# Two GNN layers on one core: the next batch's record work moved to the end of every engine's step, the sort ahead of the ranks, and 30 of 50 plain tiles read by one-hots

## The reference

```python
# layer 0
h = relu(layernorm(x))
x = x + segment_sum((h * node_vec1)[src], dst) * node_vec1_n2
# layer 1
h = relu(layernorm(x))
x = x + (1 + eps) * h + segment_sum(relu(h[src] + edge_attr), dst)
```

## Time and profile before

| what | value |
|---|---|
| median of 3 runs | 5049.15 us (5040.99 to 5050.13) |
| profiled execution | 5051.24 us, its span 5049.3 us |
| granted TensorE clock, mean | 0.899 of full speed |
| PE busy | 3734.7 us (74%) |
| DVE busy | 4209.4 us (83%) |
| POOL busy | 3745.2 us (74%) |
| ACT busy | 2165.5 us (43%) |
| layer 0, start of the first to end of the last direct step | about 160 to 3250 us of the span |

### The profile page before, as it was taken

How to read it: one execution, slowest core, us unless ns; L and a number is a source line. 1 busy time by engine, 2 the same in 40 slices (tenths; PEclk the granted TensorE clock), 3 DMA queues, 4 the chain that set the end, 5 groups by cost and what they waited for, 6 DMA issues and landing times.

```text
span 5049.3 us, 126723 instructions
## 1 busy us (share of the span) xinstructions
PE 3734.7 (74%) x43516; PEld 2830.1 (56%) x43516; DVE 4209.4 (83%) x13149; ACT 2165.5 (43%) x5783; POOL 3745.2 (74%) x3759
## 2 busy tenths in 40 slices
PE   0678878888878787888888888826666667776665
PEld 0455555565555555655555655526666666666664
DVE  9778888888888888888888888658888888888887
ACT  1344544444544454444444444423333333333332
POOL 6777777777777777777777777657777777777774
PEclk9999999999999999999999999968888888888887
DMA  6222222222222222222222221122112222222221
GB/s 105 52 52 53 52 53 52 53 52 53 52 53 52 53 52 53 52 53 52 53 52 53 52 52 29 27 68 55 48 49 53 54 55 55 55 55 55 55 55 25
DMA packets 438712, 266.11 MB, mean 53 GB/s; under 512 B 331484, under 2 KB 422732, under 8 KB 431632
## 3 DMA queue, kind: packets, MB, share of 16 engines
q1 hardware_dynamic: 317976, 185.11, 16.3%
q0 software_dynamic: 118496, 66.60, 7.5%
q10 hardware_dynamic: 1560, 5.60, 0.3%
HBM read 177.53 MB, written 79.52 MB: 51 GB/s over the span
## 4 chain that ended last, share of the span: by engine, by line
POOL 33%; DVE 22%; PE 22%; issue 18%; DMA 3%; ACT 1%; DVEq 1%; POOLq 0%; SPq 0%; ACTq 0%
POOL stage L683 24%; PE candidates L1096 14%; POOL records L693 6%; DVE arena L1534 6%; DVE arena L1515 3%; PE plain_ps L1108 3%; DVE counts L1293 2%; DMA record<-records 2%; PE candidates L1011 1%; POOL message L676 1%; PE key_rows L993 1%; DVE rank L1319 1%; DVE counts L1313 1%; DVE record L1599 1%; PE sorted_agg L1039 1%
## 5 line engine op out<-in xcount | busy, mean ns | idle before, releaser
L693 POOL DMA_INDIRECT records<-stage,place_i x1875 | 1896.8, 1012 | 607.6 <-issue 571.4
L683 POOL DMA_INDIRECT stage<-table,src_plain x1250 | 1247.4, 998 | 402.7 <-issue 380.6
L872 ACT ACTIVATE message<-candidates,member_is 128x96 bf16<-128x96 f32 x3360 | 852.1, 345 | 860.2 <-PE candidates L1096 859.9
L1534 DVE TENSOR_SCALAR arena<-window_iota,dst_rel 128x224 bf16<-128x224 f16 (+1 forms) x5000 | 1145.8, 302 | 46.0
L802 ACT ACTIVATE arena<-key_rows 125x640 f16<-125x640 f16 x1000 | 650.8, 708 | 708.6 <-DVE arena L1515 352.9
L1039 PE MATMUL sorted_agg<-arena 128*96 128x224 bf16 (+1 forms) x5000 | 629.7, 278 | 191.7 <-DVE arena L1534 191.3
L1515 DVE TENSOR_SCALAR arena<-arena,row_key 125x1280 bf16<-125x1280 f16 x1000 | 565.6, 566 | 177.7 <-ACT arena L802 138.0
L993 PE MATMUL key_rows<-ident,record 128*125 128x128 f16 x5000 | 417.4, 237 | 395.1 <-DMA record<-records 219.4
L676 POOL DMA_INDIRECT message<-table,mid_src x528 | 534.0, 1011 | 185.9 <-issue 155.4
L1039 PEld LDWEIGHTS sorted_agg<-arena 128*96 128x96 bf16 x5000 | 518.7, 132 | 219.4 <-DVE arena L1534 217.7
L993 PEld LDWEIGHTS key_rows<-ident,record 128*125 128x125 f16 x5000 | 380.8, 152 | 416.9 <-issue 330.4
(11 more groups left out here) (196 smaller groups left out, 4555.1 us busy)
## 6 DMA issues: line engine op xcount, KB each, us to landing
record<-records SPq DMA_DIRECT2D x50, 1650.0 KB, 7.2
stage<-in_edge_attr SPq DMA_DIRECT2D x125, 400.0 KB
records<-pad SPq DMA_DIRECT2D x25, 1650.0 KB
records<-stage,place_i POOLq DMA_INDIRECT x1875
stage<-table,src_plain POOLq DMA_INDIRECT x1250
message<-table,mid_src POOLq DMA_INDIRECT x528
xs<-in_x SPq DMA_DIRECT2D x8, 390.6 KB
table<-parts ACTq DMA_DIRECT2D x4, 585.9 KB
```

The source lines that it names most:

```text
L683: pool.indirect_dma_start(message[:, k, j, :] if l == 0 else rows[:, k, j, :], None, table0 if l == 0 else table1, bass.IndirectOffsetOnAx ...
L693: pool.indirect_dma_start(records, bass.IndirectOffsetOnAxis(ap=place_i[:, h, e:e + 1], axis=0), stage[:, h, e, :], None).then_inc(scatter ...
L872: last = nc.scalar.activation(direct_message[n % DB][:, m * WIDE:(m + 1) * WIDE], candidates[n % 2][:, m * WIDE:(m + 1) * WIDE], ACT.Copy, ...
L1534: last = nc.vector.tensor_scalar(dst_onehot(g, t), window_iota[:, 0:WA if tile == 0 else WT], dst_rel[:, h, tile:tile + 1], None, ALU.is_e ...
```

## The change

`BOUNDS` gets a fifteenth entry (14), so there are 30 direct tiles and 20 mid tiles; the steps hold five tiles each, and the two "arena" steps begin with a tile of 14 matmuls. The sort of batch b+1 takes the place of `rank_within` of batch b+2, which goes to where the sort stood. `prefixes` and `copy_prefix` go from the beginning of the last direct step to its last tile. On TensorE the turns of the next batch's keys leave the last direct tiles and stand behind them and behind `join_pair`; on ScalarE the copies of these keys stand behind `copy_pair`; on DVE `first_onehots` of the next batch stands behind `rank_places` and `add_pair`.

```diff
-    BOUNDS = (6, 7, 8, 8, 9, 9, 10, 10, 11, 11, 12, 12, 13, 13)
+    BOUNDS = (6, 7, 8, 8, 9, 9, 10, 10, 11, 11, 12, 12, 13, 13, 14)
-    STEPS = ((LOW, range(4, -1, -1), "far"), (LOW, range(13, 9, -1), "arena"), ...
+    STEPS = ((LOW, range(4, -1, -1), "far"), (LOW, range(14, 9, -1), "arena"), ...
 # ACT, step0
-                            if n == FIRST[5] and left_after(b) >= 2:
+                            if n == DIRECTS - 1 and left_after(b) >= 2:
                                 copy_prefix(b + 2)
-                            if n in (DIRECTS - 3, DIRECTS - 2):
-                                copy_keys(*after(b, h, u), n - (DIRECTS - 3))
...
                         copy_pair(b)
-                    if not is_last(b):
+                        copy_keys(*after(b, h, u), 0)
+                        copy_keys(*after(b, h, u), 1)
                         copy_candidates(*after(b, h, u), 0)
 # PE, step0
-                            if n == FIRST[5] and left_after(b) >= 2:
+                            if n == DIRECTS - 1 and left_after(b) >= 2:
                                 prefixes(b + 2)
                             pick_wide(b, n)
...
-                            if n in (DIRECTS - 3, DIRECTS - 2):
-                                turn_keys(*after(b, h, u), n - (DIRECTS - 3))
                         direct_products(b, DIRECTS - 1)
+                        join_pair(b)
+                        turn_keys(*after(b, h, u), 0)
+                        turn_keys(*after(b, h, u), 1)
                         pick(*after(b, h, u), 0)
-                        join_pair(b)
 # DVE, step0
                         wide_onehots(b, 4)
                         if more:
-                            rank_within(b + 2, h, u + 1)
+                            sort_rows(b + 1, 1 - h)
                         direct_onehots(b, h, 4)
                         wide_onehots(b, 5)
                         direct_onehots(b, h, 5)
                         if more:
-                            sort_rows(b + 1, 1 - h)
+                            rank_within(b + 2, h, u + 1)
                             rank_sums(b + 2)
-                        first_onehots(*after(b, h, u))
-                        if more:
                             rank_places(b + 2, h, u + 1)
                         add_pair(b)
+
+                        first_onehots(*after(b, h, u))
```

10 lines of the change are left out of this document (5 added, 5 removed).

## The result

| kernel | median | range | runs |
|---|---|---|---|
| before | 5049.64 us | 5040.99 to 5055.92 | 4 |
| changed | 5377.81 us | 5376.82 to 5379.43 | 4 |

The ratio is 1.0649 [1.0636, 1.0661]: slower by 328 us. The forecast was 5430 us, range 5350 to 5520, with 94% for slower. The sign, the place and the size of the main term were right; the forecast is 52 us too long, and nearly all of that is one term, the turn of the hardware loop from one round to the next.

The account below looks back on a forecast made before the run. It took two locked cycles, POOL's transfers and one step's compute chain through DVE and PE, as the bound. Longer steps gave +366 us, the layer's start +16.6, its end -3: +379 on 5051.2, so 5430 us, range 5350 to 5520.

Parts of the forecast that it names:

- The step's length within a round: Layer 0, prefix sums to the next prefix sums without a loop turn: 125.2 + 16.6 = 141.8 us.
- Two tiles: Direct tiles on PE, which has no idle time there: two more direct tiles lengthen each step by 6.6 us.
- the copy behind four more tiles: Prefix copy on ACT, now behind the step's last tile: the sums on DVE start 10.0 us later.
- The 28.1 us behind the sums: DVE from prefix sums to the group loop's first source one-hots: the total stays 28.1 us within a round.
- the third rival: PE resumes at half clock for some of the groups, 3 us a step: 5505 us; chance 11%.
- The loop's turn: Layer 0 where the loop turns round: 9.3 us extra, 8.0 plus 1.3 of a second wait, making a 151.1 us step.
- the branch 10 us on top: PE at the loop's branch: it stops 10 us each time, 9 times, with bounds of 0 to 10.
- Behind the last sums: Last prefix sums to the first gather: 143.9 us becomes about 141, so -3; the last batch and layer 1 cost 0.
- The record and POOL: PE's 7.65 us wait for the record goes in layer 0; POOL waits 15 to 25 us ahead of each scatter.
- POOL as the bound: Rival: POOL holds the cycle and all else fits under it, steps of 124.5 us, 4943 us; chance 4%.
- Two tiles only: Rival: only the two tiles cost, the four tiles' wait being hidden at the step's end; 5150 us; chance 8%.
- The exchange of sort and ranks: DVE, sort (10.4 us) and ranks (14.0 us) change places: the sum of its work stays the same, no cost.

Follow-up runs that it names:

- a1: The changed kernel, but with the 28 direct and 22 mid tiles of before: 5226.3 us, ratio to before 1.0347.
- b2: The kernel before, with 30 direct and 20 mid tiles only: 5156.18 us, ratio 1.0216.
- b1: The kernel before, with only the prefixes and their copy moved to the step's last direct tile: 5403.97 us, ratio 1.0707.
- b3: The kernel before, with only the next batch's key turns, key copies and first one-hots moved last: 5035.16 us, ratio 0.9976.
- b4: The kernel before, with only the next batch's sort moved ahead of the ranks on DVE: 5138.57 us, ratio 1.0181.
- a2: The changed kernel, with prefixes and their copy back at the beginning of the last direct step: 5289.97 us, ratio to before 1.0473.
- a4: The changed kernel, with the next batch's key turns, key copies and first one-hots back where before has them: 5410.7 us, ratio to before 1.0713.
- a3: The changed kernel, with 3.3 MB a batch of extra writes behind the ranks on SyncE's queue: 5977.24 us, ratio to before 1.1834.
- c1: The kernel before, with keys last and the loads of batch b+2 late: 8931.8 us on a chip where before took 8830.86 us, ratio 1.0113.
- c2: As c1, with 39 small matmuls (156 PE instructions) added in front: 8929.78 us on the same slow chip, ratio to before 1.011.
- b5: The kernel before, with loads and fills of batch b+2 held until the third group: 8841.03 us on the slow chip, ratio 1.0012.
- b6: The kernel before, with 39 small matmuls (156 PE instructions) ahead of the first batch: 8835.16 us on the slow chip, ratio 1.0003.

## Why the prediction was right, and where its size was off

**The step's length within a round: right, and for the reason given.** Two tiles +6.8 in a1 and +6.7 in b2 (forecast 6.6). The sums come 16.5 us later in the first step, and so does the step's length within a round; what is left, 9.8, is the copy behind four more tiles (forecast 10.0). a1 has these 9.8 us alone: its steps of 135.0 us against 125.2. DVE idles 10.6 us for it (forecast 10 to 14).

**The 28.1 us behind the sums: right.** Within a round 1741.44 - 1713.39 = 28.05 us pass from the sums to the group loop's first source one-hots:

```profile
1741.44 1.20 DVE L1514 TENSOR_SCALAR arena<-arena,row_key 125x1280 bf16<-125x1280 f16 x2
```

with no wait ahead of them. That PE picks late costs nothing there, and the half clock on PE's return, the third rival, adds nothing within a round either: the groups keep their 33.30 us, at a granted clock of 1.00.

**The loop's turn: the term that was mis-sized.** The prediction had "the branch 10 us on top" and "a second wait ... of which 1.3 is extra: 9.3 us where the loop turns round". Measured, it is 144.95 - 141.7 = 3.2 us. From sums to one-hots it is 1885.68 - 1855.12 = 30.6 us where 36.1 were forecast, and the second wait is not there. The nine turns take 1307.0 us in all where 1359.9 were forecast, the step that leaves the loop 141.3 where 143 were, and the twelve others 1701.5 where 1701.6 were. Together that is 54.7, the whole gap in the stretch of the sums, 3204.5 - 3149.8.

Two things in the term were wrong. The first is the size of PE's stop, 2.3 to 4.0 us in the nine turns in place of 10. The second is what bounds there. In the prediction's sum PE's chain does, with DVE waiting for the keys. Measured from the sums' start, PE begins to pick at 20.8 us (forecast 21.6) and resumes behind the branch at 24.9 (33.8), and the first keys are copied at 27.1. But DVE has destination one-hots to make until 27.9 (1883.00). So a stop of PE of 2.28 us is hidden behind DVE's work, and what lengthens the turn is DVE's own branch, 2.68 us, for which the prediction had no term. b1 and b2 have this stop of DVE in all nine turns too, 2.7 to 3.1 us, with "issue" as its releaser. Where PE's stop is longer, it shows: in a1 PE stands for 5.91 us, and the turn is 4 to 5 us longer than a step within a round.

Why is PE's stop shorter than the row of 10.00 us? The trace has the branch itself, `COMPARE_BRANCH` in L455. The view of that line gives, for PE's ten branches of layer 0, the shortest, median and longest duration in ns, before and after. The shortest is that of the tenth, which leaves the loop.

```profile
L455 PEldq COMPARE_BRANCH  x10: 83/7350/7610, 682.0 to 3000.1; - x10
```

```profile
L455 PEldq COMPARE_BRANCH  x10: 83/4696/5149, 730.1 to 3313.9; - x10
```

From the start of a taken branch to the next matmul there are two parts, the instruction and what follows it. The table has them in us for all kernels on the first chips, nine turns each; the share is that of the DMA engines over the whole of it:

| kernel | to the next matmul | the instruction | what follows | DMA share | code of |
|---|---|---|---|---|---|
| before | 9.4 to 11.1 | 6.2 to 7.6 | 3.1 to 3.8 | 0.57 to 0.63 | 28 tiles |
| b3 | 8.5 to 10.7, once 13.2 | 4.3 to 7.5 | 3.1 to 3.8, once 8.9 | 0.42 to 0.67, once 1.08 | 28 tiles |
| b4 | 7.9 to 10.8 | 4.5 to 7.6 | 3.3 to 3.9 | 0.40 to 0.62 | 28 tiles |
| b1 | 6.4 to 7.4 | 3.4 to 3.9 | 3.0 to 3.5 | 0.03 | 28 tiles |
| a1 | 7.0 to 7.6 | 3.5 to 3.9 | 3.3 to 3.9 | 0.08 to 0.10 | 28 tiles |
| b2 | 4.1 to 7.3 | 3.8 to 7.0 | 0.3 | 0.46 to 0.70 | 30 tiles |
| after | 3.8 to 5.4 | 3.4 to 5.1 | 0.3 to 0.4 | 0.08 to 0.13 | 30 tiles |
| a2 | 3.7 to 4.2 | 3.4 to 3.9 | 0.3 | 0.08 to 0.09 | 30 tiles |
| a4 | 3.7 to 5.4 | 3.4 to 5.1 | 0.3 | 0.02 to 0.05 | 30 tiles |
| a3 | 4.3 to 6.8 | 4.0 to 6.5 | 0.3 | 0.89 to 1.22 | 30 tiles |

What follows the instruction depends on where the loop's code lies. That is shown: 156 instructions in front of the same code take it from 3.2 to 3.6 us down to 0.3 (c1 to c2, which differ in nothing else, and b5 to b6, which differ in the time of the loads too). It is 3 us or more in all five kernels of 28 tiles and 0.3 in all five of 30, so the longer code of two more tiles does here what the shift does; of the 7.7 us between the stops of 10.00 and 2.28 this part is some 3. The instruction itself takes 3.4 to 5.1 us where the DMA engines are quiet, and up to 7.6 where their share is 0.4 or more. That is a correlation, not shown as the cause: a3 was to make it and gave only 1.1 us more than after, and the run that was to take it away (b5) fell on a chip where these engines are quiet at the branch without it (share 0.13 to 0.17 in b6).

The Trainium skill ("Runtime: NRT & Kernel Launch", Instruction fetch mechanics) says that a taken branch to a far target stalls on an instruction fetch. That the wait depends on the code's place, with the same work around it, agrees. The 0.1 us for a compare-and-branch in the Trainium skill ("Advanced Engine Details and Errata", Control Flow Timing), which the prediction weighed, agrees with the instruction where PE leaves the loop (0.083 us) and with DVE's (0.055 to 0.072), but not with PE's taken branch (3.4 us and more), nor with the 2.7 us for which DVE stands behind its own. By it the forecast would have been 5358, nearer to the result than mine, but only by luck: it has no stop at all on either engine.

**Behind the last sums: forecast -3, measured +0.6.** To the first plain gather it is 3574.97 - 3434.06 = 140.9 us against 143.9, so the -3 came as forecast. The rest of the execution, costed at nothing, is 3.7 us longer. Its code is the same, and among the kernels on the first chips it varies by 13 us, so nothing is read from that.

**The record and POOL: right.** PE's wait for records is gone and POOL waits 15 to 23 us ahead of the first scatter, once 13.7 (forecast 15 to 25). DVE's waits for the prefixes are 242.9 us in all, a little under the 250 to 300 of the forecast.

**The rivals.** POOL as the bound (4943): no; it waits for the places in every step. Two tiles only (5150): true of b2 alone, where the copy stands early; refuted for the whole by DVE's 10.6 us. Half clock (5505): not in the groups. But where a stop of some 4 us falls ahead of a direct tile, as in a2 and b4, the clock does cost, 1.7 us in the rows shown. The prediction was lucky there: with the prefixes late this stop does not arise.

**The exchange of sort and ranks** was costed at nothing. That DVE idles 10.6 us ahead of the sums speaks for it, but no run takes the exchange alone out of the changed kernel, so it is not shown. And it is no free move: alone it costs 91 us (b4), and in a2 its stop of 5.8 us stands against the 10.0 that an early copy would give.

## What to carry to other kernels

In a list that is held in order on each engine, ask for each cross-engine handover what stands ahead of the releasing instruction: here a 0.32 us copy, moved behind four tiles of others' work, costs 10 us in each of 23 steps (9.8 measured), though this move adds no work. A part that is moved can close a ring (late prefixes behind a key turn that waits for the record, 145.2 us) or open one (keys last), so parts measured alone need not add; only b3, which moves the waiting load behind the releasing work and leaves the release early, gains (5035.16 against 5047.79 us), and three quarters of that once, where the layer ends. And don't carry the idle time at a loop's branch from one version of a kernel to another: its length changed from 10 to 2.3 us, in part with the code's length. Ask too on which engine the stop is bare: here PE's was hidden behind DVE's work, and DVE's own was not. The releaser that a row names is to be checked against the time at which it was done.

## What the runs showed of the hardware

- A loop-back on PE costs 3.6 to 11.1 us until the next matmul, once 13.2, with nothing in the profile that it waits for. 156 instructions ahead of the loop, which do nothing for it, move that by about 3.1 us (b5 to b6, c1 to c2).
- A loop-back on DVE costs 2.7 to 3.1 us until its next instruction (after, b1, b2), though its branch instruction is over in 0.06 to 0.07 us.
- Behind a stop of PE of 3.7 to 4.4 us between full picks (a2, b4) ten matmuls of the next pick take 3.4 to 4.2 us in place of 2.19; in the two rows shown it is 3.89 us at a granted clock of 0.56.
- On the last chip PE stood idle with nothing waited for, 74 to 112 us in each step of layer 0, in all four kernels: in b5 and b6 in 43 to 53 stops, most of them between small matmuls and 0.5 to 2.6 us long, in c1 and c2 in 15 to 18, the longest 27 us. The cause is open. Two rows of b6:

```profile
2041.34 0.34 PE L1041 MATMUL sorted_agg<-arena 128*96 128x224 bf16 x1 [2.54 <-issue]
...
2044.14 0.34 PE L1041 MATMUL sorted_agg<-arena 128*96 128x224 bf16 x1 [2.46 <-issue]
```
